# A new order for layer 0's loop: row-tile products in fours, fours and key-tile sums in 10 stretches

## The chip, the cores and the metric

The kernel runs on one core of a Trainium2 chip. The metric is device time in microseconds of one launch; lower is better. The median of three runs of the kernel before is 3204.99 us.

## The reference

Two layers over x of shape (4, 1024, 128). Only layer 0 is touched:

```python
x = L0_attn_x
xn = _layernorm(x, axis=-1)
x = x + _L0_attn_ref(xn, ...) + _L0_ffn_ref(xn, ...)

# _L0_attn_ref: 16 heads of 8 channels, one shared key and value head
attn_weights = jnp.einsum('brd,bsd->brs', qr, k)
attn_probs = jax.nn.softmax(attn_weights, axis=-1)
attn_output = jnp.einsum('brs,bsd->brd', attn_probs, v)

# _L0_ffn_ref: attention with 8 heads of 128, values and outputs mixed over 8 experts by gates
xv = jnp.einsum('bsd,hedp->bshep', x, v_w.reshape(H, E, D, P))
v = jnp.einsum('bshep,bshe->bhsp', xv, gate_v)
att = jax.nn.softmax(jnp.einsum('bhqp,bhkp->bhqk', q, k) * SCALE, axis=-1)
ctx = jnp.einsum('bhqk,bhkp->bqhp', att, v)
weighted = ctx[:, :, :, None, :] * gate_o[..., None]
out = jnp.einsum('bshep,hepd->bsd', weighted, o_w.reshape(H, E, P, D))
```

## The kernel before

Layer 0 is a loop of N0 = 32 steps: 4 batches of 8. Step n does one head of the expert attention (`_L0_ffn_ref`) and two heads of the small attention (`_L0_attn_ref`). Each step works on 8 tiles of 128 tokens. Five engines each run their own list of calls, written out by hand, once per turn of `for i in range(...)`; nothing else sets the order. A call on one engine waits by semaphores for what it needs of the others. Calls with `i`, `i - 1`, `i - 2` in one turn belong to different steps: the steps are pipelined.

What TensorE does in a step, by the names of the calls:

- `values(n, t, c)`, `scores(n, t, c)`, `outputs(n, t, c)` (16 each, t = tile, c = half) and `make_y(n, c)` (2): each is three matmuls of 128x512 (`matmul3`, lines 97, 98, 99).
- `weigh(n, g)` (4): probabilities by values, line 344, 8 matmuls of 128x256, which the trace records as 16.
- `turn(n, t, h)` (16) and `turn_peaks(n, c)` (2): four transposes each (lines 332, 314).
- `peak_scores(n, t, hh, c)` (32, line 293) and `scores_by_key(n, k, hh, c)` (32, line 366): the small attention's scores by query and by key. These are row-tile products: they contract over 32 rows of the array, and `rows = slice(64 * hh + 32 * c, 64 * hh + 32 * c + 32)` puts the four combinations of hh and c on four different groups of 32 rows.
- `sum_by_key(n, k)` (8, line 381): four matmuls that use 32 columns each, recorded as 8, into a PSUM bank of their own, `sums`.

All results but those of `sum_by_key` go to a ring of seven PSUM banks (`m_ring`). `claim` takes the next bank in turn and waits until what was put there seven takes earlier has been read:

```python
        before, self.taken[k] = self.taken[k], (sem, count)
```

Who reads: VectorE reads `peak_scores` (`take_peaks`, line 1210), `values` (`gate_values`, 1223), `outputs` (`gate_outputs`, 1290), the low half of the context (`lower_ctx`, line 87, after ScalarE's `keep_ctx`, 948), and the peak rows (`shift_queries`, 1243). ScalarE reads `scores_by_key` (`exps`, 957), `turn` (`keep_turned`, 938) and `scores` (`softmax`, 928, once VectorE's `find_largest`, 1251 and 1257, has found the row's largest). `output_gates` are three short VectorE operations (1267, 1270, 1272). GpSimd adds up what was gated (`sum_values`, 849 to 851; `sum_outputs`, 858 to 862) and makes the low halves of the weights (`lower_wv`, `lower_wo`).

`batch_work(i, place)` stands at fixed places of each list and does what is done once per batch.

Of the kernel before, what the change touches and what calls it, by code (L numbers as in the profile page):

```python
# [8 lines left out]
ALU = mybir.AluOpType  # L9
# [10 lines left out]
TPB = T // P  # L20
# [159 lines left out]
def layer0(nc, whole, a, x, xnT, ident, order, combine, choice, xn_dram, listed, xs, spare, wvs, w):  # L180
# [4 lines left out]
    with ExitStack() as ctx:  # L185
# [80 lines left out]
        with nc.Block() as block:  # L266
            @block.tensor
            def _(pe):
# [189 lines left out]
                def batch_work(i, place):  # L458
# [9 lines left out]
                    if s in (4, 5) and place == 0:  # L468
                        queries(after, s - 4)
# [20 lines left out]
                for i in range(-1, N0 + 2):  # L490
                    peak_scores(i, 0, 0, 0)
                    peak_scores(i, 0, 0, 1)
                    peak_scores(i, 0, 1, 0)
                    sum_by_key(i - 2, 7)
                    scores_by_key(i - 1, 0, 0, 0)
                    scores_by_key(i - 1, 0, 0, 1)
                    scores_by_key(i - 1, 0, 1, 0)
                    scores_by_key(i - 1, 0, 1, 1)
                    scores(i - 1, 3, 0)
                    scores(i - 1, 3, 1)  # L500
                    turn(i - 1, 1, 1)
# [145 lines left out]
            def _(sp):  # L647
# [108 lines left out]
                for i in steps:  # L756
# [11 lines left out]
                    if s in (5, 6):  # L768
                        store_queries(after, s - 5)
# [1916 lines left out]
```

How the kernel before makes its waits and increments, by code:

```python
    def __call__(self, ins):  # L61
        self.n += 1
        ins.then_inc(self.sem, 1)
        self.eng.wait_ge(self.sem, self.n)
# [192 lines left out]
        def load_rden(eng, b, parts):  # L257
            eng.wait_ge(rden_stored, 16 * (b + 1))
            rden_of = rden_dram[b % 2].rearrange("(h c) (g u) -> c g h u", c=2, g=HD)
            for c in parts:
                for g in range(HD):
                    rows = slice(64 * c + HD * g, 64 * c + HD * (g + 1))
                    eng.dma_start(rden_in[rows, :, :], rden_of[c, g, :, :].partition_broadcast(HD)).then_inc(o_loaded, 16)
# [4 lines left out]
                def claim(tiles, what, sem, count):  # L269
                    tile, before = tiles.take(what, sem, count)
                    if before:
                        pe.wait_ge(*before)
                    return tile
# [1 line left out]
                def make_y(n, c):  # L275
                    if n not in steps:
                        return
                    pe.wait_ge(qk_ready, 2)
                    pe.wait_ge(x_ready, n // HS + 1)
                    ps = claim(ring, ("y", n, c), y_ready, 2 * n + c + 1)
                    matmul3(pe, ps[:, :], both(qk, slice(n % HS * D, (n % HS + 1) * D)),
                            both(xs[n // HS % 2], slice(c * 512, (c + 1) * 512))).then_inc(y_made, 1)
# [1 line left out]
                def peak_scores(n, t, hh, c):  # L284
# [2 lines left out]
                    b = n // HS  # L287
                    if t == 0 and hh == 0 and c == 0:
                        pe.wait_ge(q_split, n + 1)
                        pe.wait_ge(ks_ready, 2 * (b + 1))
```

## Time and profile before

| | |
|---|---|
| median of 3 runs | 3204.99 us (3203.18 to 3208.26) |
| span of the profiled execution (first to last instruction) | 3174.5 us |
| the median less that span (launch and end, outside the trace) | 30.5 us |
| TensorE, VectorE, ScalarE, GpSimd busy over the span | 95%, 76%, 51%, 58% |
| granted TensorE clock, mean over the span | 0.975 |

The profiled execution has no time of its own beside the span; the runs are timed apart. Times in the trace are from the span's start. Layer 0's loop fills 55 to 2600 us, layer 1 the rest. Busy TensorE is not TensorE at its peak, since the ends of matmuls are modelled: the starts are what is read below.

### The profile page before, as it was taken

What the parts mean: (1) busy time and instruction counts of PE and PEld (TensorE: products, weight loads), DVE (VectorE), ACT (ScalarE), POOL (GpSimd) and SP (SyncE); (2) the same over time, 40 slices, a digit from 0 to 9 for tenths busy, and PEclk for the clock granted to TensorE, in tenths of its full rate; (3) what the DMA queues carried; (4) which work ended last, traced back from release to release, by engine and by line L of the source; (5) the groups of instructions that cost most, each with busy time, mean ns of one, the idle gap of its engine ahead of it and who ended that gap; (6) DMA issues with size and microseconds to landing.
All of it is one profiled execution on the core that took longest, in us unless ns stands there. A gap on an engine that the chain in (4) does not pass through costs nothing. (4 is left out here: it accounts for less than half of the span.)

```text
span 3174.5 us, 51808 instructions
## 1 busy us (share of the span) xinstructions
PE 3005.8 (95%) x17486; PEld 2083.7 (66%) x17486; DVE 2399.0 (76%) x4551; ACT 1620.3 (51%) x3277; POOL 1836.4 (58%) x2277
## 2 busy tenths in 40 slices
PE   4999999999999999999999999999999977899997
PEld 2666666666666666666666666666666655566674
DVE  7888888888888888888888888888888745144343
ACT  1455555555555555555555555555555532444634
POOL 2556666666666666666666666666666634444330
PEclk7999999999999999999999999999999988899999
DMA  5000000110100011111100110011001011133322
GB/s 167 21 22 22 22 22 22 32 32 23 36 22 22 22 32 32 28 29 36 29 22 22 32 32 22 23 36 28 23 22 39 8 23 58 45 111 103 91 77 85
DMA packets 139849, 124.63 MB, mean 39 GB/s; under 512 B 28410, under 2 KB 122116, under 8 KB 139492
## 3 DMA queue, kind: packets, MB, share of 16 engines
q1 hardware_dynamic: 125892, 88.46, 10.2%
q0 software_dynamic: 10160, 30.17, 3.0%
q10 hardware_dynamic: 3536, 2.69, 0.5%
q8 instruction: 143, 2.34, 0.3%
q14 instruction: 118, 0.97, 0.1%
HBM read 97.49 MB, written 29.30 MB: 40 GB/s over the span
## 5 line engine op out<-in xcount | busy, mean ns | idle before, releaser
L1210 DVE TENSOR_REDUCE m_peaks<-m_ring 128x1 f32<-128x512 f32 x1024 | 641.0, 680 | 117.9 <-PE m_ring L293 112.6
L957 ACT ACTIVATE m_expA<-m_ring 128x512 f32<-128x512 f32 x1024 | 538.5, 602 | 370.0 <-PE m_sums L381 178.6
L849 POOL TENSOR_TENSOR m_vprod<-m_vprod 128x512 f32<-128x512 f32 x256 | 353.6, 1381 | 510.5 <-DVE m_vprod L1223 509.2
L858 POOL TENSOR_TENSOR m_oprod<-m_oprod 128x512 f32<-128x512 f32 x256 | 328.2, 1282 | 279.2 <-DVE m_oprod L1290 279.2
L928 ACT ACTIVATE m_prob<-m_ring,m_negs 128x512 f32<-128x512 f32 x512 | 347.1, 684 | 243.1 <-DVE m_negs L1257 242.9
L344 PE MATMUL m_ring<-m_probT,m_vs 128*128 128x256 f32 x2048 | 467.0, 381 | 0.0
L344 PEld LDWEIGHTS m_ring<-m_probT,m_vs 128*128 128x128 f32 x2048 | 384.3, 190 | 79.8 <-issue 27.7
L1251 DVE TENSOR_REDUCE m_negs<-m_ring 128x1 f32<-128x512 f32 x512 | 340.7, 685 | 92.9 <-PE m_ring L99 92.0
L1290 DVE TENSOR_TENSOR m_oprod<-m_ring,m_go 128x512 f32<-128x512 f32 x512 | 341.3, 686 | 56.3 <-PE m_ring L99 52.3
L1223 DVE TENSOR_TENSOR m_vprod<-m_ring,m_gate 128x512 f32<-128x512 f32 x512 | 336.6, 683 | 43.9 <-POOL m_vs L851 27.0
L938 ACT ACTIVATE m_probT<-m_ring 128x512 f32<-128x512 f32 x512 | 283.8, 598 | 57.2 <-PE m_ring L332 54.1
L332 PEld LDWEIGHTS m_ring<-k_ident,m_prob 128*128 128x128 f32 x2048 | 236.2, 142 | 83.5 <-ACT m_prob L928 31.5
L332 PE MATMUL m_ring<-k_ident,m_prob 128*128 128x128 f32 x2048 | 284.8, 276 | 4.9 <-ACT m_prob L928 3.8
L381 PE MATMUL m_sums<-m_expA,m_v 128*32 128x512 f32 x2048 | 273.6, 606 | 2.0 <-ACT m_expA L957 2.0
L97 PE MATMUL m_ring<-k_wvs,k_xs 128*128 128x512 f32 (+1 forms) x536 | 238.5, 445 | 4.7 <-POOL k_wvs L87 2.3
L293 PE MATMUL m_ring<-m_ks,m_qs 32*128 32x512 f32 x1024 | 211.9, 493 | 31.0 <-DVE m_qs L1202 29.0
L97 PE MATMUL m_ring<-k_xs,m_yT 128*128 128x512 f32 x512 | 227.1, 444 | 3.4 <-ACT m_prob L928 0.9
L97 PE MATMUL m_ring<-m_wos,m_ctxT 128*128 128x512 f32 x512 | 223.9, 437 | 5.6 <-ACT m_expA L957 2.1
L366 PE MATMUL m_ring<-m_qs,m_ks 32*128 32x512 f32 x1024 | 205.1, 483 | 11.2 <-DVE m_vprod L1223 7.2
L99 PE MATMUL m_ring<-k_wvs,k_xs 128*128 128x512 f32 (+1 forms) x536 | 212.5, 396 | 0.0
L98 PE MATMUL m_ring<-k_wvs,k_xs 128*128 128x512 f32 (+1 forms) x536 | 211.2, 394 | 0.0
L948 ACT ACTIVATE m_ctxT<-m_ring 128x256 fp32r<-128x256 f32 x128 | 49.2, 384 | 315.1 <-PE m_ring L344 315.1
(312 smaller groups left out, 5629.4 us busy)
## 6 DMA issues: line engine op xcount, KB each, us to landing
m_wraw<-in_v_w SPq DMA_DIRECT2D x32, 512.0 KB, 4.1
m_qf<-q_dram SPq DMA_DIRECT2D x128, 128.0 KB, 2.6
m_wraw<-in_o_w SPq DMA_DIRECT2D x32, 512.0 KB, 4.2
q_dram<-m_kf SPq DMA_DIRECT2D x24, 256.0 KB, 3.0
listed<-in_pad SPq DMA_DIRECT2D x6, 897.0 KB, 11.7
m_xg<-listed SPq DMA_DIRECT2D x39, 138.0 KB, 2.3
m_rows<-answers SPq DMA_DIRECT2D x8, 512.0 KB, 4.2
sums_dram<-m_sumsT ACTq DMA_DIRECT2D x128, 18.0 KB
```

Of the source, the lines that this page charges most:

```text
L97: pe.matmul(out, wh, xh, start=True, stop=False)
L332: last = pe.transpose(ps[:, c * P:(c + 1) * P], prob[t % 2][:, (4 * h + c) * P:(4 * h + c + 1) * P], ident[:, :])
L344: last = pe.matmul(ps[:, 0:2 * P], vs[n % 2][:, k, :], probT[g % 2][:, k, :], start=(k == 0), stop=(k == TPB - 1))
L849: vchain(pool.tensor_tensor(vprod[:, 0:512], vprod[:, 0:512], vprod[:, 512:1024], ALU.add))
L858: ochain(pool.tensor_tensor(op[:, 0:512], op[:, 0:512], op[:, 512:1024], ALU.add))
L928: act.activation(prob[t % 2][:, c * 512:(c + 1) * 512], ring.home["scores", n, t, c][:, :], ACT.Exp, bias=neg[t % 2], accum_out=den[n % 2] ...
L938: act.activation(probT[g % 2][:, 4 * h:4 * h + 4, (t % 2) * P:(t % 2 + 1) * P], ring.home["probT", n, t, h][:, :].rearrange("p (c q) -> p ...
L957: act.activation(expA[hh][:, c * 512:(c + 1) * 512], ring.home["scT", n, k, hh, c][:, :], ACT.Exp)\
L1210: v.tensor_reduce(peaks[:, t, hh, c:c + 1], ring.home["peaks", n, t, hh, c][:, :], AX.X, ALU.max)\
L1223: v.tensor_tensor(vprod[:, c * 512:(c + 1) * 512].rearrange("p (e d) -> p e d", e=4), ring.home["values", n, t, c][:, :].rearrange("p (e d ...
L1251: v.tensor_reduce(half_neg[:, t % 2, c:c + 1], ring.home["scores", n, t, c][:, :], AX.X, ALU.max, negate=True)\
L1290: v.tensor_tensor(oprod[t % 2][:, c * 512:(c + 1) * 512].rearrange("p (e d) -> p e d", e=4), ring.home["outputs", n, t, c][:, :].rearrange ...
```

## The change

Nothing is computed otherwise. The lists of TensorE, VectorE, ScalarE and GpSimd in the loop are written in a new order, and the loops run from -3 to N0 + 3 so that each call's `i` fits its new place. In the old list, `peak_scores` and `scores_by_key` stand in groups of one to five, with or without a `sum_by_key`, in 13 places of a step. In the new one they stand only as whole fours (all hh and c of one tile), and they and the sums are gathered in 10 places ("stretches"): six are four, sum, four; two are one four and a sum; two are a lone four. On VectorE the small join of the two halves' largest is a call of its own, `join_largest`. The queries of the next batch are projected and stored one step earlier in the batch.

The diff, cut (TensorE's list in parts, then `join_largest`, then a part of VectorE's list):

```diff
-                    if s in (4, 5) and place == 0:
-                        queries(after, s - 4)
+                    if s in (3, 4) and place == 0:
+                        queries(after, s - 3)
...
-                for i in range(-1, N0 + 2):
...
+                for i in range(-3, N0 + 4):
                     outputs(i - 2, 7, 0)
                     outputs(i - 2, 7, 1)
+                    weigh(i - 1, 0)
                     peak_scores(i, 3, 0, 0)
                     peak_scores(i, 3, 0, 1)
                     peak_scores(i, 3, 1, 0)
                     peak_scores(i, 3, 1, 1)
                     sum_by_key(i - 1, 2)
                     scores_by_key(i - 1, 3, 0, 0)
                     scores_by_key(i - 1, 3, 0, 1)
                     scores_by_key(i - 1, 3, 1, 0)
                     scores_by_key(i - 1, 3, 1, 1)
+                    turn(i - 1, 3, 0)
+                    values(i, 3, 0)
+                    peak_scores(i, 4, 0, 0)
+                    peak_scores(i, 4, 0, 1)
+                    peak_scores(i, 4, 1, 0)
+                    peak_scores(i, 4, 1, 1)
+                    turn(i - 1, 3, 1)
                     scores(i - 1, 4, 0)
+                    values(i, 3, 1)
+                    outputs(i - 1, 0, 0)
                     scores(i - 1, 4, 1)
+                    outputs(i - 1, 0, 1)
                     weigh(i - 1, 1)
+                    peak_scores(i, 5, 0, 0)
+                    peak_scores(i, 5, 0, 1)
+                    peak_scores(i, 5, 1, 0)
+                    peak_scores(i, 5, 1, 1)
+                    sum_by_key(i - 1, 3)
                     scores_by_key(i - 1, 4, 0, 0)
                     scores_by_key(i - 1, 4, 0, 1)
...
                     scores_by_key(i - 1, 4, 1, 0)
                     scores_by_key(i - 1, 4, 1, 1)
+                    turn(i - 1, 4, 0)
+                    values(i, 4, 0)
+                    outputs(i - 1, 1, 0)
...
-                    if c:
-                        v.wait_ge(half_found, 2 * k + 2)
...
+                def join_largest(n, t):
...
+                    v.wait_ge(half_found, 2 * k + 2)
...
+                    take_peaks(i + 2, 2, 1, 1)
+                    lower_ctx(i + 1, 0)
+                    take_peaks(i + 2, 3, 0, 0)
+                    take_peaks(i + 2, 3, 0, 1)
+                    take_peaks(i + 2, 3, 1, 0)
+                    output_gates(i + 1, 1)
+                    take_peaks(i + 2, 3, 1, 1)
+                    gate_values(i + 2, 3, 0)
...
+                    gate_outputs(i + 1, 0, 0)
+                    gate_values(i + 2, 3, 1)
+                    lower_ctx(i + 1, 1)
+                    gate_outputs(i + 1, 0, 1)
+                    take_peaks(i + 2, 5, 0, 0)
+                    take_peaks(i + 2, 5, 0, 1)
+                    take_peaks(i + 2, 5, 1, 0)
+                    take_peaks(i + 2, 5, 1, 1)
```

What stands on TensorE around `weigh(n, 0)` and behind it, before. L344 is `weigh`, L97 to L99 are one product of three matmuls, L293 and L366 the row-tile products, L381 a `sum_by_key`, L332 a transpose:

```order
L293 MATMUL m_ring<-m_ks,m_qs 128x512 x5
L332 MATMUL m_ring<-k_ident,m_prob 128x128 x12
L97 MATMUL m_ring<-k_wvs,k_xs 128x512
L98 MATMUL m_ring<-k_wvs,k_xs 128x512
L99 MATMUL m_ring<-k_wvs,k_xs 128x512
L381 MATMUL m_sums<-m_expA,m_v 32x512 x4
L293 MATMUL m_ring<-m_ks,m_qs 128x512 x2
L366 MATMUL m_ring<-m_qs,m_ks 128x512 x4
```

The same place of TensorE's list now, from `weigh(n, 0)` on:

```order
L344 MATMUL m_ring<-m_probT,m_vs 128x256 x8
L293 MATMUL m_ring<-m_ks,m_qs 128x512 x4
L381 MATMUL m_sums<-m_expA,m_v 32x512 x4
L366 MATMUL m_ring<-m_qs,m_ks 128x512 x4
L332 MATMUL m_ring<-k_ident,m_prob 128x128 x4
L97 MATMUL m_ring<-k_wvs,k_xs 128x512
L98 MATMUL m_ring<-k_wvs,k_xs 128x512
L99 MATMUL m_ring<-k_wvs,k_xs 128x512
L293 MATMUL m_ring<-m_ks,m_qs 128x512 x4
L332 MATMUL m_ring<-k_ident,m_prob 128x128 x4
```

The sum of tile 2 now stands between a four of peaks and a four of scores by key, right behind `weigh`; eight banks of the ring are taken there in a row, where seven exist.

What VectorE does at the next `weigh`, `weigh(n, 1)`, before. L87 is `lower_ctx`, which waits for it; L1210 reads a peak product, L1290 an output:

```order
L1251 TENSOR_REDUCE m_negs<-m_ring 128x1 x2
L1257 TENSOR_TENSOR m_negs<-m_negs 128x1
L1210 TENSOR_REDUCE m_peaks<-m_ring 128x1
L87 TENSOR_TENSOR m_ctxT<-m_ring,m_ctxT 128x256
L1210 TENSOR_REDUCE m_peaks<-m_ring 128x1 x2
L1290 TENSOR_TENSOR m_oprod<-m_ring,m_go 128x512 x3
```

And now, with line 1294 for what was 1290, and 1261 for 1257:

```order
L1261 TENSOR_TENSOR m_negs<-m_negs 128x1
L1294 TENSOR_TENSOR m_oprod<-m_ring,m_go 128x512
L1223 TENSOR_TENSOR m_vprod<-m_ring,m_gate 128x512
L87 TENSOR_TENSOR m_ctxT<-m_ring,m_ctxT 128x256
L1294 TENSOR_TENSOR m_oprod<-m_ring,m_go 128x512
L1210 TENSOR_REDUCE m_peaks<-m_ring 128x1 x4
```

`lower_ctx` and one `gate_outputs` now stand ahead of the four reads of peaks; before, a read of peaks stood ahead of `lower_ctx`, and two behind it.

## Rows read from the trace of the kernel before

**Rows 1.** Windows, 400 to 2500 us: busy PE, PEld, DVE, ACT, POOL; granted clock.

```profile
400.00:2500.00 2100.00, 2085.15 (x11298) 1429.78 (x11297) 1781.19 (x3280) 1145.33 (x2434) 1373.68 (x1738) 1.00 0.10 27
```

**Rows 2.** One line's instructions: `cut_peaks`, once per step, first and last start.

```profile
L1233 DVE TENSOR_REDUCE m_mrest<-m_peaks x32: 174/176/180, 88.3 to 2512.5; 128x16 f32<-128x32 f32 x32
```

**Rows 3.** Timeline of TensorE, a lone group: start us, us, instruction.

```profile
1311.55 0.40 PE L99 MATMUL m_ring<-m_wos,m_ctxT 128*128 128x512 f32 x1
1311.88 0.49 PE L293 MATMUL m_ring<-m_ks,m_qs 32*128 32x512 f32 x1
1311.88 0.50 PE L366 MATMUL m_ring<-m_qs,m_ks 32*128 32x512 f32 x2
1312.31 0.50 PE L97 MATMUL m_ring<-m_wos,m_ctxT 128*128 128x512 f32 x1
1312.65 0.40 PE L98 MATMUL m_ring<-m_wos,m_ctxT 128*128 128x512 f32 x1
```

**Rows 4.** Timeline of TensorE: four transposes, then products around a sum.

```profile
1353.64 0.39 PE L99 MATMUL m_ring<-k_wvs,k_xs 128*128 128x512 f32 x1
1353.88 0.60 PE L332 MATMUL m_ring<-k_ident,m_prob 128*128 128x128 f32 x4
1354.23 0.48 PE L97 MATMUL m_ring<-k_wvs,k_xs 128*128 128x512 f32 x1
1354.55 0.39 PE L98 MATMUL m_ring<-k_wvs,k_xs 128*128 128x512 f32 x1
1354.78 0.40 PE L99 MATMUL m_ring<-k_wvs,k_xs 128*128 128x512 f32 x1
1355.11 0.51 PE L293 MATMUL m_ring<-m_ks,m_qs 32*128 32x512 f32 x3
1355.54 1.07 PE L381 MATMUL m_sums<-m_expA,m_v 128*32 128x512 f32 x8
1356.54 0.90 PE L366 MATMUL m_ring<-m_qs,m_ks 32*128 32x512 f32 x4
```

**Rows 5.** Timeline of TensorE: five row-tile products with a sum; `weigh`.

```profile
1307.93 0.50 PE L366 MATMUL m_ring<-m_qs,m_ks 32*128 32x512 f32 x2
1307.94 0.71 PE L293 MATMUL m_ring<-m_ks,m_qs 32*128 32x512 f32 x3
1308.58 1.06 PE L381 MATMUL m_sums<-m_expA,m_v 128*32 128x512 f32 x8
...
1367.81 3.72 PE L344 MATMUL m_ring<-m_probT,m_vs 128*128 128x256 f32 x16
1371.18 0.58 PE L97 MATMUL m_ring<-k_wvs,k_xs 128*128 128x512 f32 x1
```

**Rows 6.** Groups by line, 60 to 2620 us: busy us, mean ns | idle before.

```profile
L444 PE MATMUL m_ring<-m_wo,m_oT 128*128 128x128 f32 x64 | 10.1, 314 | 17.1 <-POOL m_oT L806 17.1
...
L409 PE MATMUL m_ring<-k_ident,m_oT 128*128 128x128 f32 x24 | 3.4, 272 | 0.0
```

**Rows 7.** Timeline of VectorE: reads of peaks, and `lower_ctx`.

```profile
1308.53 0.69 DVE L1210 TENSOR_REDUCE m_peaks<-m_ring 128x1 f32<-128x512 f32 x1 [3.06 <-PE m_ring L293]
...
1322.26 4.26 DVE L1210 TENSOR_REDUCE m_peaks<-m_ring 128x1 f32<-128x512 f32 x7
...
1371.99 0.42 DVE L87 TENSOR_TENSOR m_ctxT<-m_ring,m_ctxT 128x256 fp32r<-128x256 f32 x1 [0.95 <-ACT m_ctxT L948]
```

**Rows 8.** Timeline of VectorE: `output_gates`, then the next `find_largest`.

```profile
1359.10 0.16 DVE L1267 TENSOR_TENSOR m_rden<-m_den 128x2 f32<-128x2 f32 x1
...
1359.59 1.28 DVE L1251 TENSOR_REDUCE m_negs<-m_ring 128x1 f32<-128x512 f32 x2
```

**Rows 9.** Waits, 400 to 2500 us: us in total, times, longest us.

```profile
DVE m_vprod L1223 <- POOL m_vs L851: 22.0, 21, 1.6
```

**Rows 10.** The page's costliest groups on GpSimd: busy us, mean ns.

```profile
L849 POOL TENSOR_TENSOR m_vprod<-m_vprod 128x512 f32<-128x512 f32 x256 | 353.6, 1381 | 510.5 <-DVE m_vprod L1223 509.2
L858 POOL TENSOR_TENSOR m_oprod<-m_oprod 128x512 f32<-128x512 f32 x256 | 328.2, 1282 | 279.2 <-DVE m_oprod L1290 279.2
```

More of the change, by code:

```diff
@@ L629, in _ @@
                     scores(i, 1, 1)
+                    make_y(i, 1)
+                    turn(i, 0, 0)
+                    values(i, 7, 1)
                     scores(i, 2, 0)
                     scores(i, 2, 1)
[L632 removed]
+                    outputs(i - 1, 3, 1)
+                    outputs(i - 1, 4, 0)
                     turn(i, 0, 1)
[L634 to L635 removed]
                     batch_work(i - 1, 1)
                     turn(i, 1, 0)
[L638 removed]
+                    weigh(i - 1, 3)
@@ new lines, in _ @@
+                    peak_scores(i + 1, 0, 0, 0)
+                    peak_scores(i + 1, 0, 0, 1)
+                    peak_scores(i + 1, 0, 1, 0)
+                    peak_scores(i + 1, 0, 1, 1)
+                    sum_by_key(i - 1, 7)
+                    scores_by_key(i, 0, 0, 0)
+                    scores_by_key(i, 0, 0, 1)
+                    scores_by_key(i, 0, 1, 0)
+                    scores_by_key(i, 0, 1, 1)
+                    turn(i, 1, 1)
+                    scores(i, 3, 0)
+                    values(i + 1, 0, 0)
@@ new lines, in _ @@
+                    values(i + 1, 0, 1)
+                    scores(i, 3, 1)
+                    outputs(i - 1, 4, 1)
+                    values(i + 1, 1, 0)
+                    sum_by_key(i, 0)
+                    scores_by_key(i, 1, 0, 0)
+                    scores_by_key(i, 1, 0, 1)
+                    scores_by_key(i, 1, 1, 0)
+                    scores_by_key(i, 1, 1, 1)
+                    turn(i, 2, 0)
+                    outputs(i - 1, 5, 0)
+                    values(i + 1, 1, 1)
@@ new lines, in _ @@
+                    outputs(i - 1, 5, 1)
+                    peak_scores(i + 1, 1, 0, 0)
+                    peak_scores(i + 1, 1, 0, 1)
+                    peak_scores(i + 1, 1, 1, 0)
+                    peak_scores(i + 1, 1, 1, 1)
+                    sum_by_key(i, 1)
+                    scores_by_key(i, 2, 0, 0)
+                    scores_by_key(i, 2, 0, 1)
+                    scores_by_key(i, 2, 1, 0)
+                    scores_by_key(i, 2, 1, 1)
+                    turn(i, 2, 1)
+                    outputs(i - 1, 6, 0)
@@ L866, in _ @@
                 add_bo(0, 1)
[L867 to L887 removed]
+                for i in range(-3, N0 + 4):
+                    sum_values(i - 2, 1)
+                    sum_outputs(i - 4, 6)
+                    lower_wo(i - 3)
+                    sum_values(i - 2, 2)
+                    sum_values(i - 2, 3)
+                    sum_outputs(i - 4, 7)
+                    sum_values(i - 2, 4)
+                    sum_outputs(i - 3, 0)
+                    sum_values(i - 2, 5)
+                    batch_work(i - 4, 0)
+                    sum_outputs(i - 3, 1)
+                    sum_values(i - 2, 6)
+                    sum_outputs(i - 3, 2)
+                    sum_outputs(i - 3, 3)
+                    lower_wv(i - 1)
+                    sum_values(i - 2, 7)
+                    batch_work(i - 3, 1)
+                    sum_values(i - 1, 0)
+                    sum_outputs(i - 3, 4)
+                    sum_outputs(i - 3, 5)
                 divide_o(B - 1, 0)
@@ L1067, in batch_work @@
                         keep_keys(after, s - 2)
-                    if s in (4, 5) and place == 0:
-                        keep_queries(after, s - 4)
+                    if s in (3, 4) and place == 0:
+                        keep_queries(after, s - 3)
                     if s == 4 and place == 2:
```

464 lines of the change are left out of this document (189 added, 275 removed).

## Prediction

> **What bounds the kernel now.** I read the windows first. In layer 0's steady part TensorE is busy 2085 of 2100 us and VectorE 1781, ScalarE 1145, GpSimd 1374, with TensorE's clock at full [rows 1]. So layer 0 lasts as long as TensorE's own list, waits on the ring included, and the change touches layer 0 alone. The step is read from one operation that stands once in it: 32 starts from 88.3 to 2512.5 us, so 2424.2 / 31 = 78.2 us [rows 2]. Then the timeline of TensorE shows what each kind of work takes, start to start; ends are modelled and overlap.
>
> Full-array matmuls of 512 columns start 0.23 us apart (1354.55, 1354.78) [rows 4], so a product of three takes 0.70. Four transposes take 0.44: 1353.88 to 1354.23, and the first matmul behind them 0.32 instead of 0.23. A `weigh` takes 1367.81 to 1371.18, and with the same 0.1 behind it about 3.46 [rows 5].
>
> Row-tile products on different rows start together (three within one merged row of 0.51 us), so a group of up to four costs about one. But every change of mode costs: into the group 0.33 instead of 0.23, from the group to the next kind 0.43, and the first matmul behind it 0.34 instead of 0.23 [rows 3]. From 1311.55 to 1312.65 are 1.10 us where two paces would be 0.47: **a lone group costs 0.63 us**. With a sum the costs are (0.33, 0.43, 1.00, and 0.43, 0.34 as above [rows 3, 4]) less the two paces: **group and sum 1.63, group, sum, group 2.06**. The sum to the products behind it is again a change of mode. A fifth product uses rows that are taken: 0.65 instead of 0.43 to the sum [rows 5], so **a second group in a row costs 0.22**.
>
> **The change, part by part.** Nothing is added or removed; the costs are of order.
>
> *Groups and modes.* Counted in the lists, a step before has 13 stretches with 20 groups and 8 sums: 4 lone groups (2.52), one double (0.85), two with a sum (3.26), five with a sum and two groups (9.25), one group, sum, group (2.06): 17.9 us. After: six group, sum, group (12.36), two with a sum (3.26), two lone (1.26): 16.9 us. **Gain 1.06 us a step.** It comes from 20 groups becoming 16 (0.9) and 35 changes of mode becoming 34 (0.2). The stretches drop by three, but most sums now have products on both sides, so that changes between products and sums rise from 9 to 14. What a change of mode costs is what the rows show at both kinds of edge alike.
>
> The Trainium skill, TensorEngine Tiling (Array Packing), Key Properties, says that a change of tiling mode, but not of the tile, drains the engine. By that rule changes of mode count, 35 against 34; by the three stretches fewer one would expect 1.9 us a step (three lone groups). The rows side with the rule.
>
> *How much of the step is waits.* 50 products 35.0, 4 `weigh` 13.8, 18 turns 7.9, stretches 17.9, and the batch work's matmuls: seven groups by line, from 10.1 to 3.4 us, in all 43 over 32 steps, 1.4 [rows 6]. That is 76.0 of 78.2: **waits before, 2.2 us a step**. After, the same sum without waits is 74.9.
>
> *The ring.* A stretch of group, sum, group takes eight banks of seven in 1.42 us. Its last product needs the bank of its first, and the three items behind it those of the other three peaks. VectorE starts to read a peak 0.60 us after the product's start (1307.94, 1308.53 [rows 5, 7]), reads one each 0.60 (seven in 4.26, one alone 0.69 [rows 7]): so the fourth is free at 0.60 + 3 x 0.60 + 0.69 = 3.1 us behind the stretch's start. TensorE wants it after 1.42 + 0.43 + 0.44 (a turn) + 0.80 (a product) = 3.1. If VectorE is free when the stretch begins and reads nothing else, there is no wait. Each thing in front of or among the four reads is one. I number the stretches from the top of TensorE's new loop, where 1 stands behind `weigh(i - 1, 0)`:
>
> - Stretches 1 and 3, behind `weigh` 0 and 1: `lower_ctx` stands in front. It starts 0.84 us behind `weigh`'s last matmul (about 1371.15; 1371.99 [rows 5, 7]), that is 0.53 behind the stretch's start, and the reads begin at 0.86: +0.26. In stretch 1 `output_gates` stands among the reads, 1359.10 to 1359.59 and the wait for its semaphores [rows 8]: 0.6. In stretch 3 a `gate_outputs` stands in front: 0.6. About 0.9 each.
> - Stretches 5 and 7: `lower_ctx` behind the first read, +0.33; in 5 two turns follow instead of turn and product, so it wants the bank 0.36 sooner. 0.7 and 0.4.
> - Stretches 4 and 9 have no `weigh` in front, in which VectorE catches up. I followed VectorE's list from the last stretch at 0.60 a read: it is about 0.9 to 1.0 us behind: 0.4 and 0.5.
> - Stretches 6 and 8: products wait for ScalarE's `softmax` of tile 7 and 3 about 0.3 and 0.2.
>
> In all 4.4 us a step, against 2.2: **loss 2.2**. I take 2.1, for some of the waits before may lie in what I called cost.
>
> *The rest at nothing.* `join_largest` on its own: VectorE's work is the same, and it has 15% idle [rows 1]; without that cover the joins' 8 x 0.3 us would be late. Storing the queries a step earlier: DMA is busy a tenth [rows 1]. The fill and drain of the pipeline have the same products, and VectorE's reads set them in both: nothing, give or take 5 us.
>
> Sum: (2.1 - 1.06) x 31 = +32 us on the profiled span of 3174.5: 3206.5, and with the 30.5 us around it (the median less that span) 3237. The median of the runs shown is where that starts.
>
> The same page of the Trainium skill, Performance Considerations, warns that tiling speeds up TensorE and not the emptying of PSUM. By the rows above the two are level at an idle VectorE; by the warning alone they would not be.
>
> **Rivals.**
> *A, the waits don't grow.* For it: VectorE has 11.9 us idle in 78.2 [rows 1], and each of my waits comes from the place of one call; if VectorE is ahead by 0.5 us more than I followed, half of them go. Then only 1.06 x 31 = 33 us are left as gain: 3172. If all waits went too, (78.2 - 74.9) x 31 = 102 us: 3103, the floor. Against it: `lower_ctx` can't start before `weigh` ends, however far ahead VectorE is. It decides where the ring's waits stay under 3.3 us a step.
> *B, GpSimd's chain.* `gate_values` of the next tile waits until `sum_values` has emptied the one `m_vprod`; that cost 22 us in 2100 before [rows 9]. In the new list five calls stand between `gate_outputs(5, 1)` and `gate_values(3, 0)`: two `sum_outputs`, two `sum_values`, `lower_wo`. Their first additions take 1.28 and 1.38 [rows 10], the smaller ones about as much again, `lower_wo` four of 256 columns about 0.7 each: some 13.6 us, where TensorE's list leaves about 14.6. If it is late by 1 us, the peaks read behind it are late too: +31 us more, 3268.
> *C, gain and loss cancel*, or the new order leaves the step as it was, since VectorE's and GpSimd's chains hold both orders: 3205.
> Doubling my waits' excess gives 3174.5 + (4.2 - 1.06) x 31 + 30.5 = 3302.
>
> **How the numbers follow.** A measurement of this kernel can tell 0.2%, 6.4 us, from no change. My forecast (2 to 70 us slower) has 0.50, A 0.27, B 0.10, C 0.13. A lies on the faster side, B on the slower; of the forecast's 0.50, 0.46 are over 6.4 us; C splits 0.03, 0.08, 0.02. Faster 0.30, same 0.12, slower 0.58. The predicted time is the forecast's, 3237; the range takes in A's 3172 and a bit of its way to the floor, and B, 3155 to 3285, with a tenth left out on either side.
>
> **What the profile after would show.** The operation once per step 79.2 us apart. Lone groups at 0.63 and 0.43 to the next kind, whatever is next. In stretch 3, the last of the second four about 0.7 us behind the first three, and the item that takes the bank of the fourth peak about 1 us late; waits of TensorE's loads on `m_peaks` grown from those of before; VectorE idle before `lower_ctx` as before. It is wrong if full fours cost more than 0.43, if VectorE reads peaks faster than 0.60 apart, or if the stretches show no such waits.

## The result, and the profile after

The changed kernel takes **3344.94 us** (median of 4 runs, 3335.84 to 3353.35) where the kernel before takes 3205.23 us beside it (4 runs, 3203.18 to 3208.26): a ratio of **1.0423, 95% interval 1.0395 to 1.0451**. It is slower, as forecast, but by 140 us where 32 were forecast, and outside the range.

The first view is the operation that stands once in a step, then the window of the steady part and the page's head, of the changed kernel.

```profile
L1233 DVE TENSOR_REDUCE m_mrest<-m_peaks x32: 174/175/178, 90.3 to 2650.2; 128x16 f32<-128x32 f32 x32
```

```profile
400.00:2500.00 2100.00, 2013.10 (x10663) 1363.17 (x10662) 1727.24 (x3097) 1075.40 (x2311) 1290.32 (x1632) 0.99 0.09 25
```

```profile
span 3334.0 us, 51818 instructions
```

The starts run from 90.3 to 2650.2, so a step lasts 2559.9 / 31 = 82.6 us; it was 78.2 [rows 2]. All four engines do less in the same 2100 us than before [rows 1], TensorE 72 us less and 635 matmuls fewer: no engine has become the bound, TensorE waits more. 4.4 us a step by 31 steps are 136 us, of the size of the whole result of 140.

Where layer 1 starts is seen at its first kind of matmul (the line moved from L1846 to L1857 with the diff); the first row is of the kernel before, the second of the changed one.

```profile
L1846 PE MATMUL m_ring<-k_spare,m_kT x256: 372/374/791, 2644.4 to 3064.6; 32*128 32x256 f32 x128
```

```profile
L1857 PE MATMUL m_ring<-k_spare,m_kT x256: 372/374/787, 2771.4 to 3223.8; 32*128 32x256 f32 x128
```

Layer 0 ends 127.0 us later. From there to the end of the span are 530.1 us in the profile before and 562.6 in the one after, though nothing in layer 1 changed. This is no effect of the change: one and the same kernel, run twice (e9_batch_moved and e12_batch_moved_again below), has 528 and 568 us there on two chips, with a layer 0 of the same length, and the old order too has 534 us there in one run (e10_parts) and 574 in another (e4_light_before). The changed kernel's profiled execution took 3335.84 us with a span of 3334.0, so launch and end outside the trace are 1.8 us. The rest of the "30.5 us around it", called launch and end ahead of the prediction, is a profile of before whose layer 1 was some 30 us shorter than in the runs beside it: right in the sum, and not what it was called.

What the engines waited for, 400 to 2500 us (us in all, times, longest), first one line of the kernel before, then the changed kernel:

```profile
ACT m_prob L928 <- DVE m_negs L1257: 204.0, 159, 4.7
```

```profile
ACT m_prob L928 <- DVE m_negs L1261: 354.4, 179, 4.6
DVE m_ctxT L87 <- ACT m_ctxT L948: 88.7, 47, 2.4
DVE m_vprod L1223 <- POOL m_vs L851: 86.1, 51, 3.0
PEld m_ring L366 <- ACT m_prob L928: 54.8, 73, 1.4
PEld m_ring L293 <- DVE m_peaks L1210: 36.9, 60, 1.3
```

Two waits have grown beside the ring's waits on `m_peaks`. VectorE's `gate_values` waits 86.1 us for GpSimd, where it was 22.0 [rows 9], and ScalarE's `softmax` waits 354.4 us for VectorE's joined largest, where it was 204.0; behind it TensorE waits in turn for `m_prob`.

**Stretch 3**, whose waits the prediction worked out call by call. First TensorE, then VectorE, of the changed kernel:

```profile
1303.80 0.50 PE L293 MATMUL m_ring<-m_ks,m_qs 32*128 32x512 f32 x4
1304.24 1.06 PE L381 MATMUL m_sums<-m_expA,m_v 128*32 128x512 f32 x8
1305.23 1.26 PE L366 MATMUL m_ring<-m_qs,m_ks 32*128 32x512 f32 x4
1306.69 0.63 PE L332 MATMUL m_ring<-k_ident,m_prob 128*128 128x128 f32 x4 [0.20 <-DVE m_peaks L1210]
1307.20 0.50 PE L97 MATMUL m_ring<-k_wvs,k_xs 128*128 128x512 f32 x1
```

```profile
1304.33 0.42 DVE L87 TENSOR_TENSOR m_ctxT<-m_ring,m_ctxT 128x256 fp32r<-128x256 f32 x1 [2.44 <-ACT m_ctxT L948]
1304.67 0.68 DVE L1294 TENSOR_TENSOR m_oprod<-m_ring,m_go 128x512 f32<-128x512 f32 x1
1305.27 2.48 DVE L1210 TENSOR_REDUCE m_peaks<-m_ring 128x1 f32<-128x512 f32 x4
```

`lower_ctx` starts 0.53 us behind the stretch's start, as predicted, and the reads begin 1.47 behind it (0.86 and 0.6 were predicted). The first bank is free at 1305.27 + 0.69 = 1305.96, and the last product of the second four starts at about 1306.0: its row reads 1.26 us instead of 0.5 because that one started late. The turn waits for the second read, the next `values` for the third (1305.27 + 0.60 + 0.60 + 0.69 = 1307.16; it starts at 1307.20). Without waits 0.43 + 1.00 + 0.43 + 0.44 = 2.30 lie between 1303.80 and that `values`, and it took 3.40: 1.1 us late, where 0.9 was predicted. The mechanism stands there as described.

**Stretch 8**, where it does not. GpSimd, VectorE, ScalarE and TensorE of the changed kernel, around the third tile:

```profile
1343.12 1.27 POOL L858 TENSOR_TENSOR m_oprod<-m_oprod 128x512 f32<-128x512 f32 x1 [7.21 <-DVE m_oprod L1294]
1344.46 1.06 POOL L859 TENSOR_TENSOR m_oprod<-m_oprod 128x256 f32<-128x256 f32 x1
1345.60 1.31 POOL L860 TENSOR_TENSOR m_oprod<-m_oprod 128x128 f32<-128x128 f32 x1
1346.99 0.46 POOL L862 TENSOR_TENSOR k_x<-k_x,m_oprod 128x128 f32<-128x128 f32 x1
1347.41 2.80 POOL L87 TENSOR_TENSOR k_wvs<-m_wraw,k_wvs 128x256 fp32r<-128x256 f32 x4
1350.16 1.30 POOL L849 TENSOR_TENSOR m_vprod<-m_vprod 128x512 f32<-128x512 f32 x1
1351.54 0.74 POOL L850 TENSOR_TENSOR m_vprod<-m_vprod 128x256 f32<-128x256 f32 x1
1352.36 0.46 POOL L851 TENSOR_TENSOR m_vs<-m_vprod 128x128 f32<-128x128 f32 x1
```

```profile
1344.97 1.63 DVE L1202 SCALAR_TENSOR_TENSOR m_qs<-m_qs,m_split,m_qf 128x1024 fp32r<-128x1024 f32 x1
...
1348.25 1.88 DVE L1210 TENSOR_REDUCE m_peaks<-m_ring 128x1 f32<-128x512 f32 x3
1352.95 1.29 DVE L1223 TENSOR_TENSOR m_vprod<-m_ring,m_gate 128x512 f32<-128x512 f32 x2 [2.83 <-POOL m_vs L851]
1354.16 1.28 DVE L1251 TENSOR_REDUCE m_negs<-m_ring 128x1 f32<-128x512 f32 x2
1355.47 0.16 DVE L1261 TENSOR_TENSOR m_negs<-m_negs 128x1 f32<-128x1 f32 x1
```

```profile
1355.67 0.69 ACT L928 ACTIVATE m_prob<-m_ring,m_negs 128x512 f32<-128x512 f32 x1 [4.25 <-DVE m_negs L1261]
```

```profile
1354.96 0.49 PE L366 MATMUL m_ring<-m_qs,m_ks 32*128 32x512 f32 x1
1356.50 0.50 PE L366 MATMUL m_ring<-m_qs,m_ks 32*128 32x512 f32 x3 [1.04 <-ACT m_prob L928]
```

Read it from the bottom. TensorE's four products of stretch 8 start as one and three, 1.54 us apart, since the second needs a bank that `softmax` has yet to empty. `softmax` waited 4.25 us for the join (`m_negs`), the join stands behind two `gate_values` and two `find_largest`, and `gate_values(0)` had to wait 2.83 us for GpSimd, whose `sum_outputs` of tile 3, `lower_wv` and `sum_values` of tile 7 fill 1343.12 to 1352.8 without a gap. The prediction's sum has 0.2 us for `softmax` in stretch 8, and nothing for the chain behind it.

### The profile page after: what moved, and what is told of

It is laid out like the page before. It is cut to its first block and busy times, and to the rows that moved or that the text cites. A ratio compares the mean times of both kernels' runs of the same rounds, so it can differ in the third digit from the quotient of the medians.

```text
span 3334.0 us, 51818 instructions
## 1 busy us (share of the span) xinstructions
PE 3044.1 (91%) x17486; PEld 2085.9 (63%) x17486; DVE 2451.4 (74%) x4551; ACT 1608.0 (48%) x3277; POOL 1838.1 (55%) x2277
## 5 line engine op out<-in xcount | busy, mean ns | idle before, releaser
L1210 DVE TENSOR_REDUCE m_peaks<-m_ring 128x1 f32<-128x512 f32 x1024 | 649.4, 682 | 46.6 <-PE m_ring L293 46.1
L849 POOL TENSOR_TENSOR m_vprod<-m_vprod 128x512 f32<-128x512 f32 x256 | 327.6, 1280 | 633.1 <-DVE m_vprod L1223 632.2
L957 ACT ACTIVATE m_expA<-m_ring 128x512 f32<-128x512 f32 x1024 | 553.5, 607 | 250.8 <-PE m_ring L366 250.8
L1223 DVE TENSOR_TENSOR m_vprod<-m_ring,m_gate 128x512 f32<-128x512 f32 x512 | 348.6, 686 | 184.3 <-POOL m_vs L851 104.2
L344 PE MATMUL m_ring<-m_probT,m_vs 128*128 128x256 f32 x2048 | 462.9, 379 | 0.3 <-ACT m_probT L938 0.3
L344 PEld LDWEIGHTS m_ring<-m_probT,m_vs 128*128 128x128 f32 x2048 | 386.0, 190 | 55.7 <-ACT m_probT L938 0.7
L332 PE MATMUL m_ring<-k_ident,m_prob 128*128 128x128 f32 x2048 | 315.8, 279 | 36.1 <-DVE m_peaks L1210 28.0
L938 ACT ACTIVATE m_probT<-m_ring 128x512 f32<-128x512 f32 x512 | 308.3, 617 | 70.4 <-PE m_ring L332 70.4
L332 PEld LDWEIGHTS m_ring<-k_ident,m_prob 128*128 128x128 f32 x2048 | 229.6, 141 | 160.9 <-issue 98.3
L381 PE MATMUL m_sums<-m_expA,m_v 128*32 128x512 f32 x2048 | 273.2, 606 | 1.2 <-ACT m_expA L957 1.0
L366 PEld LDWEIGHTS m_ring<-m_qs,m_ks 32*128 32x128 f32 x1024 | 93.2, 181 | 280.5 <-issue 148.8
L366 PE MATMUL m_ring<-m_qs,m_ks 32*128 32x512 f32 x1024 | 214.2, 495 | 40.1 <-ACT m_prob L928 22.8
L97 PE MATMUL m_ring<-k_wvs,k_xs 128*128 128x512 f32 (+1 forms) x536 | 230.4, 430 | 2.6 <-DVE m_yg L2240 1.1
L97 PE MATMUL m_ring<-k_xs,m_yT 128*128 128x512 f32 x512 | 218.8, 427 | 10.0 <-ACT m_prob L928 9.5
L97 PE MATMUL m_ring<-m_wos,m_ctxT 128*128 128x512 f32 x512 | 221.6, 433 | 6.1 <-DVE m_oprod L1294 5.2
L99 PE MATMUL m_ring<-k_wvs,k_xs 128*128 128x512 f32 (+1 forms) x536 | 214.1, 399 | 0.0
L859 POOL TENSOR_TENSOR m_oprod<-m_oprod 128x256 f32<-128x256 f32 x256 | 202.3, 790 | 20.1
```

The lines of the kernel that those rows point to most:

```text
L97: pe.matmul(out, wh, xh, start=True, stop=False)
L332: last = pe.transpose(ps[:, c * P:(c + 1) * P], prob[t % 2][:, (4 * h + c) * P:(4 * h + c + 1) * P], ident[:, :])
L344: last = pe.matmul(ps[:, 0:2 * P], vs[n % 2][:, k, :], probT[g % 2][:, k, :], start=(k == 0), stop=(k == TPB - 1))
L849: vchain(pool.tensor_tensor(vprod[:, 0:512], vprod[:, 0:512], vprod[:, 512:1024], ALU.add))
L938: act.activation(probT[g % 2][:, 4 * h:4 * h + 4, (t % 2) * P:(t % 2 + 1) * P], ring.home["probT", n, t, h][:, :].rearrange("p (c q) -> p ...
L957: act.activation(expA[hh][:, c * 512:(c + 1) * 512], ring.home["scT", n, k, hh, c][:, :], ACT.Exp)\
```

## Theories and experiments

T1: the ring. What was lost is what the prediction named, VectorE's reads of peaks behind other calls and banks that come free too late, only more. T2: GpSimd's chain, as read above. T3: the new order is longer by something that has to do with neither, for example what its groups cost. Times of these runs stand beside a kernel before of 3175 to 3220 us, by the chip and its layer 1; so I compare ratios (the changed kernel's is 1.0423), and for layer 0 the step, by the first and last start of L1233 as above.

| kernel | us | ratio, 95% interval | step, us |
|---|---|---|---|
| before (its profile) | | 1 | 78.2 |
| changed | 3344.94 | 1.0423, 1.0395 to 1.0451 | 82.6 |
| e1_sum_first | 3321.02 | 1.0322, 1.0302 to 1.0343 | 81.7 |
| e2_reads_first | 3322.53 | 1.0321, 1.0302 to 1.034 | 81.7 |
| e3_both | 3286.2 | 1.0209, 1.0189 to 1.0228 | 80.6 |
| e4_light_before | 3193.39 | 0.9922, 0.9904 to 0.9939 | 77.4 |
| e5_light_both | 3200.29 | 0.9941, 0.9919 to 0.9964 | 78.0 |
| e6_six_banks_before | 3409.14 | 1.0581, 1.0555 to 1.0608 | 84.6 |
| e7_six_banks_after | 3697.92 | 1.1492, 1.1463 to 1.1522 | 93.7 |
| e8_weigh_behind | 3624.61 | 1.1258, 1.1233 to 1.1284 | 91.4 |
| e9_batch_moved | 3260.5 | 1.0268, 1.0253 to 1.0283 | 81.1 |
| e10_parts | 3171.25 | 0.999, 0.9981 to 1.0 | 78.2 |
| e11_both_again | 3282.1 | 1.0227, 1.0187 to 1.0268 | 80.4 |
| e12_batch_moved_again | 3296.92 | 1.0269, 1.0229 to 1.0309 | 81.2 |

**e1_sum_first**: GpSimd's list alone is changed, so that what `gate_values` waits for comes first.

```diff
-                    sum_outputs(i - 3, 3)
-                    lower_wv(i - 1)
                     sum_values(i - 2, 7)
+                    lower_wv(i - 1)
+                    sum_outputs(i - 3, 3)
```

> The new order, with GpSimd's list changed at one place: sum_values of tile 7, then lower_wv, then sum_outputs of tile 3 (instead of sum_outputs, lower_wv, sum_values). Theory T1 (the loss is banks of the ring that VectorE and ScalarE give back late behind the stretches): no change, 3345 us. Theory T2 (a good part of the loss is GpSimd's chain: VectorE stands 2.8 us for sum_values of tile 7 and joins of tile 3 come late, so that scores_by_key of tile 1 waits 1.5 us for softmax): the stand is gone and the step gets 1.3 to 1.7 us shorter, 40 to 50 us in all, about 3300.

The step falls from 82.6 to 81.7 us and the ratio by 0.010. Of the waits, 400 to 2500 us, the one of `gate_values` on GpSimd is back at its level of before ([rows 9]):

```profile
DVE m_vprod L1223 <- POOL m_vs L851: 20.7, 26, 0.8
PEld m_ring L366 <- ACT m_prob L928: 28.5, 53, 0.8
```

T2 is right in kind: 0.8 us a step, 26 us, hang on the order of three calls on an engine that is busy 61% of the time. It is smaller than the 1.3 to 1.7 expected. The stand of 2.8 us is not gone but shorter: once a step VectorE now stands 1.2 us ahead of the same `gate_values`, which starts 0.09 us behind the end of the product of TensorE that it reads (26 such waits between 400 and 2500 us, 24 of them of 1.2 us). How much of VectorE's waiting reaches TensorE through `softmax` was not measured. The edit also moves GpSimd's additions away from VectorE's cast of the queries, which takes 0.73 us instead of 1.39 (last section); the run doesn't part the two.

**e2_reads_first**: VectorE's list alone, in stretches 1 and 3: the reads come ahead of what stood in front of or among them.

```diff
-                    lower_ctx(i + 1, 0)
                     take_peaks(i + 2, 3, 0, 0)
+                    lower_ctx(i + 1, 0)
                     take_peaks(i + 2, 3, 0, 1)
                     take_peaks(i + 2, 3, 1, 0)
-                    output_gates(i + 1, 1)
                     take_peaks(i + 2, 3, 1, 1)
+                    output_gates(i + 1, 1)
...
-                    lower_ctx(i + 1, 1)
                     gate_outputs(i + 1, 0, 1)
                     take_peaks(i + 2, 5, 0, 0)
+                    lower_ctx(i + 1, 1)
```

> The new order, with VectorE's list changed at two places: behind weigh 0 the first peak is read ahead of lower_ctx and output_gates comes after the fourth; behind weigh 1 gate_outputs and the first peak are read ahead of lower_ctx. T1: of the two waits of about 0.9 to 1.1 us a step in stretches 1 and 3, some 0.6 and 0.5 go, so 1.1 x 31 = 35 us, about 3310. T2: no change, 3345.

0.9 us a step, 27 us, where T1 expected 1.1: T1 is right too, and is not the whole.

**e3_both**: the two edits together.

> The edits of e1 and e2 together. T1 and T2 both hold: they lie in different parts of the step, so the gains add, about 3345 - 45 - 35 = 3265. If one of them only moves the wait elsewhere, no better than the other alone.

The step falls by 2.0 us where 0.8 and 0.9 make 1.7; the two losses are separate, and somewhat more than add. 2.4 us a step over before remain.

**e4_light_before and e5_light_both**: VectorE's reads of the peaks are made cheap, in the old order and in that of e3_both. They look at 128 of a bank's 512 columns, so that the largest is taken over a quarter of the scores.

```diff
-                    v.tensor_reduce(peaks[:, t, hh, c:c + 1], ring.home["peaks", n, t, hh, c][:, :], AX.X, ALU.max)\
+                    v.tensor_reduce(peaks[:, t, hh, c:c + 1], ring.home["peaks", n, t, hh, c][:, 0:128], AX.X, ALU.max)\
```

> The kernel before, where take_peaks reads only the first 128 of a bank's 512 columns: the largest of a quarter of the keys, so the small attention's shift is not the full one; everything else as before. VectorE gets some 12 us a step lighter. T1: the ring's waits on VectorE that the order before has (1.6 of 76.2 us in its steps without batch work) nearly go, 78.2 to about 76.8, 3160. If the old order doesn't wait on VectorE, no change, 3205.

> The kernel of e3 (new order, both edits) with take_peaks reading only the first 128 of 512 columns, as in e4: the small attention's shift is not the full one. T1 (what is left of the loss is banks that VectorE gives back late): the rest of it goes, and the smaller number of groups shows: a step without batch work at 73.5 to 75 us against e4's 75.8, the mean at 76.5 to 77 against 77.6, so 20 to 35 us below e4's time, about 3165. Theory T3 (fours side by side with a sum cost TensorE more by themselves): it stays above e4, at 3220 or more.

The old order gains 0.8 us a step, the new one 2.6 (80.6 to 78.0). So after both repairs the new order still pays 1.8 us a step more than the old for VectorE's pace; with that taken away only 0.5 us is left between them, and T3 is small. The reads of the peaks are where that pace tells most: TensorE's waits that the profile puts down to `m_peaks` (400 to 2500 us) fall from 56.8 us in e3 to 8.3 in e5, which is 1.9 us a step. But a read takes 0.28 us instead of 0.68, 32 times a step, so VectorE is earlier at all its other calls too, and these runs don't part the two.

What T1 expected of e5 came out for the shortest step (next paragraph) and not for the mean, which was to fall to 76.5 to 77 us, under that of e4, and came to 78.0. What T3 expected, 3220 us or more, did not come out either: 3200.29. In the old order the light reads gave 0.8 where the expectation had 1.4 and the prediction had put 2.2 us a step down as waits on the ring: if that 2.2 is right, most of those don't hang on the reads of peaks.

The shortest steps of the steady part, one near the end of each batch, tell more (starts of `turn_peaks` in the trace): 75.8 us in e4 and 75.0 in e5. There the order of fours is 0.8 us the faster, as the groups' count wants. The mean step lies 1.8 us above the shortest in e4 and 3.0 in e5: the rest is lost in the other steps, where the batch work stands. In the kernels with full reads the same difference is 2.0 us before (shortest 76.4) and 2.7 in the changed one (79.9), 0.7 more, and 3.2 in e3 (77.4).

**e6_six_banks_before and e7_six_banks_after**: one bank fewer in the ring, in both orders.

```diff
-        ring = Ring([m.psum(f"ring{k}", [P, 512]) for k in range(7)])
+        ring = Ring([m.psum(f"ring{k}", [P, 512]) for k in range(6)])
```

> The kernel before with six banks in the ring instead of seven. T1: the old order waits more too, since each bank is wanted one item earlier, but has five products at most in a row: 1 to 2 us a step, 3240 to 3270 where before is 3205 to 3220. T3: banks don't matter in either order, no change.

> The new order with six banks instead of seven. T1: eight banks are taken in 1.4 us in six places of a step, and with one bank fewer each of these waits for one more read of VectorE, 0.6 us: 3.6 us a step on top, about 110 us, 3455. That is more than twice what the old order loses. T3: no change, 3345.

The old order loses 6.4 us a step, the new one 11.1. So the two are 9.0 us apart with six banks and 4.4 with seven; with both repairs in the new order they are 2.4 apart, and 0.5 where VectorE's reads are light. That is T1's own sign: the order costs what the ring lacks. Both were expected to lose far less, 1 to 2 us and 3.6, and the new one more than twice what the old one does; it is 1.7 times. The old order lives close to its seven banks as well, which the rows of waits on `m_peaks` alone did not show.

**e8_weigh_behind**: on top of e3_both, the four `weigh` stand behind the stretches 1, 3, 5 and 7 instead of in front, on TensorE (`lower_ctx` and `keep_ctx` behind the reads and exponentials accordingly), so that VectorE would have 3.5 us in which to empty the four peaks.

```diff
-                    weigh(i - 1, 0)
                     peak_scores(i, 3, 0, 0)
...
                     scores_by_key(i - 1, 3, 1, 1)
+                    weigh(i - 1, 0)
                     turn(i - 1, 3, 0)
```

> The kernel of e3 with each weigh moved from in front of its stretch of group, sum, group to behind it, and VectorE's lower_ctx and ScalarE's keep_ctx behind the reads of the fours. T1: weigh is one item of 3.5 us, in which VectorE reads the four peaks, and lower_ctx no longer stands in front of them: the waits of stretches 1, 3, 5 and 7 that are left in e3, about 2.2 us a step, go: 3286 - 68 = 3218, at the kernel before or just under or over it. T3: the number of modes and groups is the same, so no change from e3, 3286.

The expectation fails by far: 91.4 us a step. The waits, 400 to 2500 us, and the window (the clock is the number 0.94):

```profile
DVE m_ctxT L87 <- ACT m_ctxT L948: 356.8, 91, 6.0
PEld m_ring L293 <- DVE m_peaks L1210: 68.8, 40, 3.9
PEld m_ring L293 <- DVE m_qs L1202: 58.2, 22, 2.8
```

```profile
400.00:2500.00 2100.00, 1915.72 (x9532) 1278.69 (x9532) 1551.86 (x2787) 971.22 (x2066) 1154.14 (x1457) 0.94 0.08 23
```

The products of the peaks now wait for `split_queries` (L1202), which `weigh` 3 had covered, and for banks of earlier work that VectorE empties during a `weigh`. I read it so, that a `weigh` in front of a stretch is where VectorE catches up, and that the three microseconds behind the stretch do not replace it; the run moved calls on three engines at once and shows no more than that this place is worse.

**e9_batch_moved**: on top of e3_both, to see what the batch work's share is.

```diff
                     cut_peaks(i + 2)
-                    batch_work(i, 6)
-                    batch_work(i, 7)
                     find_largest(i + 2, 0, 0)
...
                     gate_outputs(i + 1, 4, 0)
+                    batch_work(i, 6)
+                    batch_work(i, 7)
                     split_queries(i + 3)
```

> The changed kernel with both repairs (GpSimd's sums ahead of the weights' copies, the reads of peaks ahead of what stood among them; 1.0209 of the kernel before), and now the two calls of batch work that stand on VectorE between cut_peaks and the first find_largest moved seven calls down, to just ahead of split_queries. The product whose bank that find_largest empties starts 0.4 us a step late on average, all of it in steps with batch work. Theory, that the share of batch work in the loss is VectorE's calls standing ahead of what TensorE waits for: 0.4 x 31 = 12 us less, ratio 1.0170. Rival, that the delay only moves to split_queries, since VectorE's work in those steps is the same: ratio 1.020 to 1.022. A second rival, that the join of the third tile or split_queries is late next, and the turn of the peaks with it: over 1.022.

The second rival holds: the step grows from 80.6 to 81.1 us. VectorE, then TensorE, in a step with batch work:

```profile
1480.57 2.28 DVE L1322 TENSOR_SCALAR k_spare<-k_x,m_mean,m_rstd 128x128 f32<-128x128 f32 x4
1482.78 1.23 DVE L83 CAST m_qs<-m_qf 128x1024 fp32r<-128x1024 f32 x1
1484.04 1.62 DVE L1202 SCALAR_TENSOR_TENSOR m_qs<-m_qs,m_split,m_qf 128x1024 fp32r<-128x1024 f32 x1
```

```profile
1485.72 0.51 PE L293 MATMUL m_ring<-m_ks,m_qs 32*128 32x512 f32 x4 [1.84 <-DVE m_qs L1202]
```

The product behind the moved calls is on time again (0.78 us to the next instead of about 1.2 on average), and the peaks of the next tile wait for the queries instead, 1.84 us here; the part of TensorE's list around them takes 9.1 us on average instead of 8.3. At both places that were tried for these calls something waits.

**e10_parts**: `join_largest` as a call of its own and the queries a step earlier, in the old order. The join's lines leave `find_largest` and become a call behind it, here for the first tile:

```diff
                     find_largest(i, 0, 1)
+                    join_largest(i, 0)
...
-                    if s in (5, 6):
-                        store_queries(after, s - 5)
+                    if s in (4, 5):
+                        store_queries(after, s - 4)
```

> The old order with the two small parts of the change alone: join_largest as a call of its own, straight behind the second find_largest of its tile, and the queries' products and stores a step earlier. The work and the order of all else are those of the kernel before. The prediction put both at nothing: ratio 0.999 to 1.001. Rival, that the earlier queries collide with the products and the logits of the same group of steps: one step in eight longer by up to 3 us on each of four groups, 12 us, ratio 1.004.

No change, 78.2 us a step. Both edits cost nothing in the old order, as predicted; in the new one they were not tried apart.

**e11_both_again and e12_batch_moved_again**: e3_both and e9_batch_moved once more, side by side on one chip, since they had run beside kernels before of 3219 and 3175 us.

> The kernel of e3_both once more, unchanged, beside the next one on the same chip, since e3_both and e9_batch_moved ran beside kernels before whose times differ by 1.4%. If that difference lies in layer 1 alone, the step of layer 0 lasts 80.6 to 80.8 us by its profile again, on whichever chip. Ratio 1.021 to 1.023.

> The kernel of e9_batch_moved once more, unchanged. That a wait on split_queries takes more than the move gives back: a step of 81.1 to 81.3 us, some 17 us more than e11_both_again, a ratio 0.005 higher than its. If the two are level here, the cost of the move was the chip's.

Steps of 80.4 and 81.2 us, as before, and 14.8 us between the medians where 17 were expected: the cost of the move is not the chip's. The start of layer 1 in the two profiles of the same kernel (e9, span 3257.0; e12, span 3298.4):

```profile
L1857 PE MATMUL m_ring<-k_spare,m_kT x256: 372/374/791, 2729.1 to 3146.6; 32*128 32x256 f32 x128
```

```profile
L1857 PE MATMUL m_ring<-k_spare,m_kT x256: 372/374/791, 2730.8 to 3188.2; 32*128 32x256 f32 x128
```

Layer 0 agrees within 2 us, and layer 1 lasts 527.9 us on one chip and 567.6 on the other. Much of it lies in one place: from 2760 to 2790 us TensorE is busy 21.7 us in the first profile and 4.9 in the second. What starts that wait the profile doesn't name, so the cause stays open.

No version with all of its work is faster than the kernel before.

## Why the prediction was right or wrong

*Which side.* Right, and in good part by the mechanism named: waits for the ring that outweigh the gain of the groups. More than half of what was missed lies elsewhere, in the two steps below that failed.

*Groups and modes, gain 1.06.* Right within 0.3: 0.8 us a step between the shortest steps of e5 and e4, where least else interferes. In the trace after, a four leads to the next kind in 0.44 us (1303.80, 1304.24), as a group of three did in 0.43 [rows 3]. By the stretches it would have been 1.9, so the changes of mode are what to count; here the Trainium skill, TensorEngine Tiling (Array Packing), Key Properties, by which a change of mode drains the engine, and the runs agree, though e5 changes more than that count.

*The ring, net 2.1.* The mechanism is right and the term too small by 0.6. (Its parts add up to 4.3 and not to 4.4, which changes nothing here.) Reads behind other calls in stretches 1 and 3 cost 0.9 (e2), VectorE's pace 1.8 more than in the old order (e4 and e5 against 78.2 and e3): 2.7, at most, since the light reads help VectorE elsewhere too. In stretch 3 the walk gives 0.9 and the trace 1.1. The Trainium skill, TensorEngine Tiling (Array Packing), Performance Considerations, warns that tiling speeds up TensorE and not the emptying of PSUM; e4 and e5, where the emptying is quicker, and e6 and e7, with a bank less, agree with it.

*"Rival B, GpSimd's chain."* This is the step that failed first. The chain was walked in one place, between `gate_outputs(5, 1)` and `gate_values(3, 0)`, found to fit, and left at a chance of 0.10. The chain that binds stands one round earlier (`sum_outputs` 3, `lower_wv`, `sum_values` 7), and its sum from [rows 10] and the smaller additions was never made: it takes 9.7 us, from 1343.12 to 1352.8, and VectorE wants its end 7.0 us behind its start (1350.13, when its reads are done). It costs 0.8 to 1.1 us a step (e1 alone, and e3 against e2), where the sum had nothing.

*"The batch work's matmuls ... 1.4."* Second failure. Batch work was counted on TensorE alone and taken as the same in both orders. But the steps with batch work lose more in the new order: the mean step lies 1.8 us above the shortest in e4 and 3.0 in e5, 1.2 more, and 0.7 more in the changed kernel itself, where the shortest steps lose as well. That batch calls on VectorE stand ahead of something that TensorE wants is seen at two of them, in e9, where their place alone is worth 0.4 us in one part of the step and 0.8 in another; for the rest of the 1.2 it is argued.

Together: -0.8 + 0.9 + 1.8 + 0.8 to 1.1 + 1.2 = 3.9 to 4.2 of the 4.4 us a step. Taken as differences between runs, 4.4 is 2.0 (both repairs) + 1.8 or 1.9 (light reads, new order less old) + 0.5 (e5 less e4, which is -0.8 in the shortest steps and the rest elsewhere); the remainder of the first sum is mostly what the two repairs give more together than apart. That this closes is arithmetic and confirms no cause; what the clock has in each term is not known (below).

*Nothing for join, queries, fill and drain.* e10 shows it for the first two, in the old order. Fill and drain came out 9 us shorter (the 31 steps grew by 136, the start of layer 1 came 127 later), where 5 either way were allowed.

*Rivals A and C* are out. *"Doubling my waits' excess", 3302*, was the nearest number given. The range took each error as apart from the others. I take them to have one cause, that VectorE and GpSimd are late together, which no run tests; then its upper end was too near.

## What to carry to other kernels

An order that bunches work on one engine takes its slack from the ring, so count how many banks a bunch takes in what time and walk the engine that frees them, call by call; and where two engines hand buffers back to each other, make the same walk for every round trip in the step, not for the one that looks longest. Steps with extra work need a walk of their own, on the engines that free buffers. Time that an engine spends on work that takes few buffers (here `weigh`) is where the others can catch up; here it was better ahead of a bunch than behind (e8, one try).

## What the runs showed of the hardware

TensorE's granted clock falls to half behind some of the waits. Windows of the changed kernel ahead of, in and behind one such stretch (the clock is the third number from the end), then TensorE within it:

```profile
768.00:775.00 7.00, 5.96 (x32) 3.65 (x30) 4.07 (x10) 2.77 (x7) 5.19 (x7) 1.00 0.30 85
776.70:780.10 3.40, 3.40 (x12) 2.14 (x10) 2.48 (x6) 1.28 (x3) 1.77 (x4) 0.50 0.00 0
780.10:785.00 4.90, 4.77 (x31) 2.45 (x28) 4.07 (x8) 2.56 (x5) 4.15 (x5) 1.00 0.00 0
```

```profile
773.39 0.49 PE L366 MATMUL m_ring<-m_qs,m_ks 32*128 32x512 f32 x1
774.92 0.50 PE L366 MATMUL m_ring<-m_qs,m_ks 32*128 32x512 f32 x3 [1.04 <-ACT m_prob L928]
...
777.41 0.63 PE L98 MATMUL m_ring<-k_wvs,k_xs 128*128 128x512 f32 x1
777.84 0.63 PE L99 MATMUL m_ring<-k_wvs,k_xs 128*128 128x512 f32 x1
```

The clock is at 1.2 instead of 2.4 GHz from 776.7 to 780.1, after a wait of the kind that ends GpSimd's chain (1.53 us between starts), and full-array matmuls start 0.43 us apart instead of 0.23. Between 400 and 2500 us the changed kernel has 12 such stretches, 44 us in all, and the kernel before has 2, 7 us in all (from 1044.2 and 2071.6), which its window's 1.00 [rows 1] rounds away. At half pace a stretch costs at most half its length, so that the new ones there are at most 19 of the some 112 us that layer 0 loses in that time, an estimate. Not every wait of this size brings one, and no run here parts the clock from the waits behind which it falls. In e8, with the longest waits, the mean clock is 0.94.

GpSimd's additions and VectorE's splitting of the queries (L83 and L1202, 1024 columns each) stretch each other. In stretch 8 GpSimd's addition of 256 columns takes 1.06 us and the one of 128 takes 1.31 from 1344.46 on, and 0.74 and 0.46 from 1351.54 on. Over the whole run (shortest, median, longest ns), first before, then after: GpSimd's first addition of `sum_values`, its smallest of `sum_outputs`, and VectorE's cast.

```profile
L849 POOL TENSOR_TENSOR m_vprod<-m_vprod x256: 1264/1282/2271, 56.4 to 2525.9; 128x512 f32<-128x512 f32 x128
L860 POOL TENSOR_TENSOR m_oprod<-m_oprod x256: 452/458/468, 135.5 to 2597.6; 128x128 f32<-128x128 f32 x128
L83 DVE CAST m_qs<-m_qf x32: 685/695/1779, 53.1 to 2448.8; 128x1024 fp32r<-128x1024 f32 x32
```

```profile
L849 POOL TENSOR_TENSOR m_vprod<-m_vprod x256: 1258/1277/1320, 59.7 to 2664.7; 128x512 f32<-128x512 f32 x128
L860 POOL TENSOR_TENSOR m_oprod<-m_oprod x256: 453/461/1326, 149.0 to 2733.0; 128x128 f32<-128x128 f32 x128
L83 DVE CAST m_qs<-m_qf x32: 687/1386/1395, 53.1 to 2580.8; 128x1024 fp32r<-128x1024 f32 x32
```

Both orders bring the two together about once a step, and GpSimd's additions are 46 us longer by it in 2100 us in either. What the order moves is the place. In the old one the addition of 512 columns takes up to 2.27 us; in the new one it is the chain of stretch 8 that is 1.2 us longer, and VectorE's cast takes 1.39 us in most steps, where it took 0.70. This is seen in the rows and was not tried apart. The Trainium skill, SBUF — State Buffer, Who interferes with whom, has an operation of VectorE with two inputs in SBUF and one of GpSimd that reads SBUF exclude each other for a whole instruction. The rows agree nearly: L1202 ends at 1344.97 + 1.63 = 1346.60, and the addition of L860 that began at 1345.60 ends at 1346.91, 0.31 behind it, where it takes 0.46 when nothing is beside it.
